# Attention with experts: softmax inverses and root guesses on ScalarE, root refinement on GpSimd, all q/k scaling on VectorE, input rows two batches ahead

## The chip, the cores and the metric

The kernel runs on one core of a Trainium2 chip. A core has five engines that run their own instruction queues side by side and meet through semaphores: TensorE (PE, matrix products), VectorE (DVE), ScalarE (ACT), GpSimd (POOL) and SyncE (SP, which here only issues DMAs). The metric is the time of one execution on the device, in microseconds (us); lower is better. Three runs of the kernel before took 1273.59, 1277.20 and 1277.99 us, median 1277.2 us.

## The reference, cut to what matters

16 batches of 256 tokens of width 256; 16 heads of 64 columns.

```
shift = silu(t) @ W_ada.T + b_ada
h = _ln(x, ln1_g, ln1_b) + shift
qkv = (h @ Wqkv.T).reshape(b, n, 3, H, HD)
q = _ln(qkv[:, :, 0].transpose(0, 2, 1, 3), qn_g, qn_b)      # mean and root over each head's 64 columns
k = _ln(qkv[:, :, 1].transpose(0, 2, 1, 3), kn_g, kn_b)
attn = softmax(einsum(q, k) / 8);  o = attn @ v
x = x + o @ Wout.T
gate = softmax(tok @ Wgate.T)                                # tok: all 4096 rows
vals, idx = top_k(gate.T, 512)                               # 512 rows for each of 8 experts
g = _ln(tok[idx], mlp_g, mlp_b)
y = gelu(g @ fc1 + b1s) @ fc2 + b2s
tok = tok.at[idx].add(y * vals)
```

`_ln` divides by sqrt(variance + 1e-5). The softmax divides by the sum of 256 exponentials.

## The kernel before, in words

The program has three parts. Attention runs to about 983 us of the span, the choice of rows for the experts to about 1072 us, and the eight experts to the end. The change touches the first part and one small piece of the second.

**Units.** `over_batches` walks over batches; each has eight units, `hp` 0 to 7, one for each pair of heads (`u` counts them all). Every engine has its own `batch` function with the same walk, and each queue's order is the order in which its function is written. Entries -1 and B (16) start and drain the pipeline; batches 2 to 14 are one loop body, the others are written out. In unit `hp`, TensorE transposes q and k of pair `hp+1` (L1272), forms a projection chunk of 512 columns in three passes (L452 to L454), multiplies the probabilities of pair `hp-1` by v (L1294) and sums them with a matrix of ones (L1298), forms the scores of pair `hp` (L1310, L1319), the rough scores of pair `hp+1` for their row maximum (L1330), and a second chunk. `CHUNKS` says which units have chunks: 0, 3, 4 and 7 a q and a k chunk each, 1 and 5 two v chunks, 2 and 6 none. Unit 0 has besides the output projection of the previous batch. Of the projected q and k, unit 7 of one batch and unit 0 of the next make one group (pairs 0 to 3), units 3 and 4 the other (pairs 4 to 7).

**Dividing by the softmax sum.** VectorE waits for the sum (`attended`), takes its reciprocal from PSUM into `rec` (L1147), multiplies (`oT`, L1149, which sets `divided`) and rounds a copy (`o_hi`, L1153); GpSimd forms the rest `o_lo` (L928). TensorE's next L1294 writes the same bank `av`, so it waits for `divided` of the unit before.

**Roots.** ScalarE copies each q or k chunk (`raw`, L966) and squares it (`sq`, L968); VectorE sums the squares by head (L1105). At the end of units 0 and 4, VectorE adds up `var` (L1189, L1191) and runs `rsqrt`: a guess from the bits and three Newton steps, eleven dependent instructions on 128x34 or 128x36 elements (L1023 to L1031). In units 1 and 5, after the maximum `m` (L1169), the four chunks of the group are scaled (`times_rstd`, L831): three on VectorE, one on GpSimd (`POOL_CHUNKS`). TensorE asks for them in units 3 and 7 (`qn_ready`, `qn_pool_ready` before L1272).

**Rows.** The same roots carry the variances of the batch's input rows (`xh`, L1139: x of the batch after, in unit 1) and of its result rows (`xh2`, L1089, unit 5, printed as xh in the profile). `sync_batch` loads `x_sb` one batch ahead. In the second part `last_rows` (L1093) does the same for the last batch, between the one-hot tables and the row lists.

Of the kernel before, what the change touches and what calls it, by code (L numbers as in the profile page):

```python
# [28 lines left out]
P = 128  # L29
# [20 lines left out]
NEWTON = 3  # L50
FIRST_LOOPED, LAST_LOOPED = 2, B - 2
# [26 lines left out]
def make_counts():  # L78
# [8 lines left out]
    for b in range(-1, B + 1):  # L87
# [53 lines left out]

class Need:
# [11 lines left out]
def over_batches(eng, batch):  # L154

    batch(-1, cur=False, nxt=True, prv=False)
    batch(0, cur=True, nxt=True, prv=False)
    batch(1, cur=True, nxt=True, prv=True)
    with eng.Fori(FIRST_LOOPED, LAST_LOOPED + 1) as b:
        batch(b, cur=True, nxt=True, prv=True)  # L160
    batch(B - 1, cur=True, nxt=False, prv=True)
    batch(B, cur=False, nxt=False, prv=True)


def build(nc, x, condT, w_adaT, vecs, w_qkvT, w_outT, w_gateT, experts, b2s, consts, out):
    ctx = ExitStack()
    with ctx:
# [38 lines left out]
        var_half = sb("var_half", [P, NH + 4], I32)  # L206
        ny = sb("ny", [P, NH + 4])
# [126 lines left out]
        tanh_done = sem("tanh_done")  # L334
# [27 lines left out]
        chunk_summed = sem("chunk_summed")  # L362
        rstd_ready = sem("rstd_ready")
        hT_split = sem("hT_split")
# [3 lines left out]
        dve_step = sem("dve_step")  # L368
        free_sem = {"act": act_read, "dve": dve_read}
# [150 lines left out]
        def phase23_pool(pool):  # L520
# [5 lines left out]
            nc.gpsimd.tensor_tensor(flat(w2_lo[0]), w2, flat(w2_hi[0]).bitcast(F32), ALU.subtract).then_inc(first_w2_lo_ready, 1)  # L526
            pool.wait_ge(index_ready, 1)
# [30 lines left out]
        def phase23_scalar(act):  # L558
# [22 lines left out]
            split_w2(0)  # L581
            act.wait_ge(first_transposed, 1)
# [243 lines left out]
        POOL_CHUNKS = 1  # L826

        def times_rstd(eng, par, c):

            r = rstd[par][:, c * 8:(c + 1) * 8].rearrange("p (h o) -> p h o", o=1).to_broadcast([P, 8, HD])  # L830
            return eng.tensor_tensor(qn[par][:, c, :].rearrange("p (h d) -> p h d", d=HD),  # L831
                                     raw[:, c, :].rearrange("p (h d) -> p h d", d=HD), r, ALU.mult)

        def sync_batch(sp):
            need = Need(sp)

            def batch(b, cur, nxt, prv):
                if nxt and not (isinstance(b, int) and b < 0):
                    need(xh_ready, b + 1)
                    sp.dma_start(x_sb[:, :, :], x[bass.ds(b + 1, 1)].rearrange("o (t p) d -> p (o t) d", p=P)  # L840
                                 if not isinstance(b, int) else x[b + 1].rearrange("(t p) d -> p t d", p=P)).then_inc(x_in, 16)
# [35 lines left out]
        def _(pool):  # L877
            need = Need(pool)
            nc.gpsimd.memset(ones[:, :], 1.0).then_inc(ones_ready, 1)
# [18 lines left out]
            def batch(b, cur, nxt, prv):  # L898
                def normalise(hp, c):

                    par = 1 if hp == 0 else 0
                    g = b * 2 + (1 if hp == 0 else 2)
                    if c == 0:
                        need(rstd_ready, through("newton", b, hp))
                        need(qk_transposed, (g - 1) * GU)
                    ins = times_rstd(nc.gpsimd, par, c)
                    if c == POOL_CHUNKS - 1:
                        ins.then_inc(qn_pool_ready, 1)

                for hp in range(UNITS):  # L910
# [13 lines left out]
                    if (cur and hp > 1) or (hp == 0 and prv):  # L924

                        for pair in ((hp - 2,) if hp else (UNITS - 2, UNITS - 1)):
                            need(normed, u - 1 if pair != UNITS - 1 else u)
                            nc.gpsimd.tensor_tensor(o_lo[:, pair, :], oT[pair % 2][:, :], o_hi[:, pair, :].bitcast(F32), ALU.subtract).then_inc(o_split, 1)  # L928
                    if hp == 1 and cur:
                        normalise(0, 0)  # L930
                    if hp == 5 and nxt:
                        normalise(4, 0)
# [4 lines left out]
            phase23_pool(pool)  # L937
# [3 lines left out]
        def _(act):  # L941
            need = Need(act)
            act.wait_ge(cond_in, 48)
# [462 lines left out]
```

## Time and profile before

| | value |
|---|---|
| median of three runs | 1277.2 us (1273.59 to 1277.99) |
| the profiled execution | 1278.72 us |
| its span in the trace | 1276.9 us |
| busy: TensorE, VectorE, ScalarE, GpSimd | 1102.1, 1050.9, 625.0, 565.7 us |
| share of the span | 86%, 82%, 49%, 44% |
| chain that ended last, by engine | TensorE 67%, VectorE 22%, issue 6% |
| granted TensorE clock, mean | 0.949 |

Busy time is the union of an engine's instructions; waiting is not in it. "Chain" is the path of work followed back from the last instruction: at each step to what released it. The duration of an instruction overlaps the next one's by about a tenth of a microsecond, so where instructions stand back to back, the distance of their starts is the better measure. A duration that is many times the shortest of its kind has a wait in it that the profiler does not show apart.

### The profile page before, as it was taken

The numbers are of one execution on the slowest core, as the hardware profiler recorded it, in microseconds if no ns is written. First come the engines' busy times: TensorE is split into PE (matmuls) and PEld (weight loads), VectorE is DVE, ScalarE is ACT, GpSimd is POOL, SyncE is SP. The second block draws the span as 40 slices with busy tenths as digits, with TensorE's granted clock in tenths as the row PEclk, the third lists the DMA queues.
The fourth block names the chain that finished last, engine by engine and source line by source line (L and its number), as shares of the span: only waits on it lengthen the run. The fifth ranks groups of instructions, "written<-read, shape, count | busy, mean of one in ns | idle before, by whom it ended". The sixth has DMA issues, their size and how long they took to land.

```text
span 1276.9 us, 24531 instructions
## 1 busy us (share of the span) xinstructions
PE 1102.1 (86%) x8291; PEld 849.3 (67%) x8291; DVE 1050.9 (82%) x1967; ACT 625.0 (49%) x1000; POOL 565.7 (44%) x507
## 2 busy tenths in 40 slices
PE   4689999999999999999999999999986015999996
PEld 3457676767767676767677676767664014898995
DVE  8688988888888989888888889898886884777773
ACT  4445655555464655555554646555541101544541
POOL 2465544454454545444444545444552203335423
PEclk9799999999999999999999999999998555999998
DMA  4000000000001000000000000000001403346412
GB/s 173 9 1 18 17 18 17 16 16 16 16 16 33 9 24 16 16 16 16 16 16 19 14 33 15 18 16 16 9 18 41 146 1 126 100 108 173 118 19 31
DMA packets 32277, 48.50 MB, mean 38 GB/s; under 512 B 7920, under 2 KB 28528, under 8 KB 30960
## 3 DMA queue, kind: packets, MB, share of 16 engines
q1 hardware_dynamic: 26096, 39.49, 9.5%
q0 software_dynamic: 6144, 8.52, 3.6%
q8 instruction: 23, 0.38, 0.1%
q14 instruction: 14, 0.11, 0.0%
HBM read 35.29 MB, written 12.71 MB: 38 GB/s over the span
## 4 chain that ended last, share of the span: by engine, by line
PE 67%; DVE 22%; issue 6%; ACT 1%; DMA 1%; POOL 0%; DVEq 0%; SPq 0%; ACTq 0%; POOLq 0%
PE ch L452 12%; PE ch L453 10%; PE ch L454 10%; PE av L1294 8%; PE sc L1319 7%; PE sc L1310 4%; DVE rec L1147 4%; PE av L1298 3%; PE pq L1272 3%; DVE qn L831 3%; PE mx L1330 2%; DVE var L1189 2%; DVE hit L706 1%; PE sc L452 1%; PE sc L453 1%
## 5 line engine op out<-in xcount | busy, mean ns | idle before, releaser
L923 POOL TENSOR_TENSOR qk_lo<-qkT,qk_hi 128x512 fp32r<-128x512 f32 x128 | 165.1, 1290 | 272.5 <-ACT qk_hi L989 272.5
L1147 DVE RECIPROCAL rec<-av 128x256 f32<-128x256 f32 x128 | 224.6, 1755 | 45.3 <-PE av L1298 44.8
L1001 ACT ACTIVATE prob<-sc 128x1024 f32<-128x1024 f32 x128 | 131.4, 1027 | 236.2 <-PE sc L1319 236.2
L918 POOL TENSOR_TENSOR prob_sum<-prob 128x512 f32<-128x512 f32 x128 | 165.0, 1289 | 140.5 <-ACT prob L1001 140.5
L452 PE MATMUL ch<-w_hi,hT_lo 128*128 128x512 f32 x384 | 173.8, 452 | 7.5 <-DVE w_lo L1069 7.2
L1294 PE MATMUL av<-prob,V 128*64 128x256 f32 x1024 | 141.0, 396 | 43.4 <-DVE oT L1149 41.0
L1169 DVE TENSOR_REDUCE m<-mx 128x4 bf16<-128x1024 f32 x128 | 155.5, 1214 | 0.0
L453 PE MATMUL ch<-w_lo,hT_hi 128*128 128x512 f32 x384 | 153.8, 401 | 0.0
L454 PE MATMUL ch<-w_hi,hT_hi 128*128 128x512 f32 x384 | 152.8, 398 | 0.0
L1294 PEld LDWEIGHTS av<-prob,V 128*64 128x64 f32 x1024 | 65.6, 137 | 101.2 <-issue 81.1
L1105 DVE TENSOR_REDUCE ssum<-sq 128x8 f32<-128x512 f32 x128 | 84.8, 680 | 54.8 <-ACT sq L968 53.0
L983 ACT ACTIVATE qkT<-pq,vec 128x256 f32<-128x256 f32 x128 | 72.2, 564 | 100.6 <-PE pq L1272 100.6
L928 POOL TENSOR_TENSOR o_lo<-oT,o_hi 128x256 fp32r<-128x256 f32 x128 | 94.6, 739 | 24.2 <-DVE o_hi L1153 24.2
L966 ACT ACTIVATE raw<-ch 128x512 f32<-128x512 f32 x128 | 75.4, 589 | 56.1 <-PE ch L454 55.9
L551 POOL DMA_INDIRECT out<-yout,index x32 | 52.3, 1634 | 106.3 <-DVE yout L822 99.9
L452 PEld LDWEIGHTS ch<-w_hi,hT_lo 128*128 128x128 f32 x384 | 73.2, 191 | 30.2 <-issue 8.3
L1272 PE MATMUL pq<-con,qn 128*128 128x128 f32 x512 | 79.3, 278 | 12.5 <-DVE qn L831 12.5
L1310 PE MATMUL sc<-neg_ident,m 128*128 128x256 bf16 x512 | 78.9, 277 | 12.1 <-issue 9.3
L454 PEld LDWEIGHTS ch<-w_hi,hT_hi 128*128 128x128 f32 x384 | 73.6, 192 | 19.6
L1319 PE MATMUL sc<-qk_hi,qk_lo 64*128 64x256 f32 x512 | 86.4, 334 | 0.0
L989 ACT ACTIVATE qk_hi<-qkT 128x512 fp32r<-128x512 f32 x128 | 80.7, 630 | 11.6
L595 ACT ACTIVATE yT<-ch,b_sb 128x512 f32<-128x512 f32 x64 | 44.1, 688 | 86.2 <-PE ch L454 86.1
(196 smaller groups left out, 2749.3 us busy)
## 6 DMA issues: line engine op xcount, KB each, us to landing
fcw<-experts SPq DMA_DIRECT2D x8, 2048.0 KB, 9.1
x_sb<-x SPq DMA_DIRECT2D x16, 256.0 KB, 2.8
xr_sb<-x SPq DMA_DIRECT2D x16, 256.0 KB, 2.7
out<-tok SPq DMA_DIRECT2D x16, 256.0 KB, 2.2
rows_dram<-xh SPq DMA_DIRECT2D x16, 256.0 KB, 2.2
prob<-w_qkvT SPq DMA_DIRECT2D x2, 512.0 KB, 8.2
qn<-w_qkvT SPq DMA_DIRECT2D x2, 512.0 KB, 9.0
V<-w_qkvT SPq DMA_DIRECT2D x2, 512.0 KB, 8.3
```

What stands on the lines that cost most here:

```text
L452: nc.tensor.matmul(psum, l_lo, r_hi, start=first, stop=False)
L453: nc.tensor.matmul(psum, l_hi, r_lo, start=False, stop=False)
L454: return nc.tensor.matmul(psum, l_hi, r_hi, start=False, stop=last)
L918: nc.gpsimd.tensor_tensor(prob_sum[(hp - 1) % 2][:, :, :], pr[:, :, 0, :], pr[:, :, 1, :], ALU.add).then_inc(prob_summed, 1)
L923: nc.gpsimd.tensor_tensor(qk_lo[par][:, :], qkT[par][:, :], qk_hi[par][:, :].bitcast(F32), ALU.subtract).then_inc(lo_ready, 1)
L1001: nc.scalar.activation(prob[hp % 2][:, :], sc[:, :], ACT.Exp, scale=HD ** -0.5).then_inc(prob_ready, 1)
L1147: chain(nc.vector.reciprocal(rec[:, :], av[:, N:2 * N]))
L1169: nc.vector.tensor_reduce(m[(hp + 1) % 2][:, :], mx[:, :].rearrange("p (a j) -> p a j", a=4), AX.X, ALU.max).then_inc(max_ready, 1)
L1272: ins = nc.tensor.transpose(pq[:, at * P:(at + 1) * P], qn[gpar][:, c, i * P:(i + 1) * P], ident)
L1294: nc.tensor.matmul(av[hh * HD:(hh + 1) * HD, 0:N], V[gpar][:, jt, i * P + hh * HD:i * P + (hh + 1) * HD], prob[(hp - 1) % 2][:, at:at + N] ...
L1310: nc.tensor.matmul(both[:, :, it, :], m[par][:, hh * TT + it:hh * TT + it + 1].to_broadcast([P, P]), neg_ident[:, :].rearrange("p (o n) -> ...
L1319: ins = nc.tensor.matmul(sc[:, at:at + N], k_part[par][rows, keys], q_part[par][rows, 0:N], start=False, stop=(k_part is qk_hi and q_part ...
```

## The change

- **Inverse of the softmax sum.** ScalarE waits for `attended`, takes the logarithm of the sum (`log_sum`) and then the exponential of its negative (`rec`). VectorE multiplies the sum by `rec` in place in PSUM (`error`), multiplies the product by `rec` (`o_raw`), and forms (error - 2) * o_raw: one Newton step, with the sign turned. The sign is taken back by a subtraction where `tok` is formed. The rounded copy `o_hi` is made by ScalarE, after `prob`.
- **Roots.** VectorE writes half the variance plus half of 1e-5, once, for all 36 columns; ScalarE guesses the inverse root by a logarithm and an exponential (`power_guess`); GpSimd makes one Newton step in four instructions (`refine`). All four chunks are scaled by VectorE (`normalise`), group (b,0) at the end of unit 0 instead of unit 1, group (b,4) still in unit 5.
- **Order.** On VectorE the maximum `m` stands between the two head sums of a unit instead of behind both. Result rows move from unit 5 to unit 6.
- **Rows ahead.** The statistics of x are taken in unit 3 for the batch after the next, and `xh` is written in unit 6; `x_sb` is loaded two batches ahead. The loop body covers batches 2 to 13.
- **Start and end.** silu of the condition uses an exponential and VectorE's reciprocal instead of a tanh; the last rows' root goes the same way through ScalarE and GpSimd.

```
-                        chain(nc.vector.reciprocal(rec[:, :], av[:, N:2 * N]))
+                        need(o_split, u - 2)
+                        need(inverse_ready, u)
                         o = oT[(hp - 1) % 2]
-                        nc.vector.tensor_tensor(o[:, :], av[:, 0:N], rec[:, :], ALU.mult).then_inc(divided, 1)
-                        nc.vector.tensor_copy(o_hi[:, (hp - 1) % UNITS, :], o[:, :]).then_inc(normed, 1)
+                        nc.vector.tensor_tensor(av[:, N:2 * N], av[:, N:2 * N], rec[:, :], ALU.mult).then_inc(error_done, 1)
+                        nc.vector.tensor_tensor(o_raw[:, :], av[:, 0:N], rec[:, :], ALU.mult).then_inc(rough_done, 1)
+                        need(error_done, u)
+                        need(rough_done, u)
+                        nc.vector.scalar_tensor_tensor(o[:, :], av[:, N:2 * N], 2.0, o_raw[:, :], ALU.subtract, ALU.mult).then_inc(divided, 1)
...
# ScalarE, in every unit, around prob
+                        need(attended, u)
+                        need(divided, u - 1)
+                        nc.scalar.activation(log_sum[:, :], av[:, N:2 * N], ACT.Ln).then_inc(log_done, 1)
+                        need(log_done, u)
+                        nc.scalar.activation(rec[:, :], log_sum[:, :], ACT.Exp, scale=-1.0).then_inc(inverse_ready, 1)
                     if cur:
                         nc.scalar.activation(prob[hp % 2][:, :], sc[:, :], ACT.Exp, scale=HD ** -0.5).then_inc(prob_ready, 1)
+                        need(divided, u)
+                        nc.scalar.activation(o_hi[:, (hp - 1) % UNITS, :], oT[(hp - 1) % 2][:, :], ACT.Copy).then_inc(o_hi_ready, 1)
...
+            def power_guess(b, hp, extra=0):
+                need(var_ready, count)
+                need(rstd_ready, count - 1)
+                nc.scalar.activation(log_var[:, 0:n], var[:, 0:n], ACT.Ln, scale=2.0).then_inc(log_var_done, 1)
+                need(log_var_done, count)
+                nc.scalar.activation(guess[:, 0:n], log_var[:, 0:n], ACT.Exp, scale=-0.5).then_inc(guess_ready, 1)
...
+            def refine(b, hp, extra=0):
+                need(guess_ready, count)
+                nc.gpsimd.tensor_tensor(a, y, y, ALU.mult).then_inc(pool_step, 1)
+                nc.gpsimd.tensor_tensor(a, a, v, ALU.mult).then_inc(pool_step, 1)
+                nc.gpsimd.tensor_tensor(a, three_halves[:, 0:n], a, ALU.subtract).then_inc(pool_step, 1)
+                need(qn_ready, b * 2 + (0 if hp == 0 else 1))
+                nc.gpsimd.tensor_tensor(dst, a, y, ALU.mult).then_inc(rstd_ready, 1)
...
+            def normalise(b, hp):
+                need(rstd_ready, through("newton", b, hp))
+                need(qk_transposed, (g - 1) * GU)
+                for c in range(4):
+                    ins = times_rstd(1 if hp == 0 else 0, c)
+                ins.then_inc(qn_ready, 1)
```

Three places of the queues are shown, all in batch 1, which is written out and has the loop's order. VectorE before, in unit 4, from the division to the start of the root:

```order
L1147 RECIPROCAL rec<-av 128x256
L1149 TENSOR_TENSOR oT<-av,rec 128x256
L1153 CAST o_hi<-oT 128x256
L1105 TENSOR_REDUCE ssum<-sq 128x8 x2
L1169 TENSOR_REDUCE m<-mx 128x4
L1189 TENSOR_SCALAR var<-ssum 128x32
L1191 TENSOR_SCALAR var<-mv 128x2
L1023 TENSOR_SCALAR var_half<-var 128x36
L1024 TENSOR_SCALAR ny<-var_half 128x36
```

The same stretch of VectorE's queue now, from the second instruction of the division on, with unit 5 behind it:

```order
L1217 TENSOR_TENSOR o_raw<-av,rec 128x256
L1220 SCALAR_TENSOR_TENSOR oT<-av,o_raw 128x256
L1178 TENSOR_REDUCE ssum<-sq 128x8
L1235 TENSOR_REDUCE m<-mx 128x4
L1178 TENSOR_REDUCE ssum<-sq 128x8
L1258 TENSOR_SCALAR var<-mv 128x4
L1261 TENSOR_SCALAR var<-ssum 128x32
L1216 TENSOR_TENSOR av<-av,rec 128x256
L1217 TENSOR_TENSOR o_raw<-av,rec 128x256
L1220 SCALAR_TENSOR_TENSOR oT<-av,o_raw 128x256
L1235 TENSOR_REDUCE m<-mx 128x4
L860 TENSOR_TENSOR qn<-raw,rstd 128x512 x4
```

The eleven instructions of the root and the rounded copy are gone from it, and the two multiplications and the subtraction of each unit stand in the place of the reciprocal.

ScalarE's queue before, in unit 4:

```order
L983 ACTIVATE qkT<-pq,vec 128x256
L985 ACTIVATE qkT<-pq,vec 128x256
L989 ACTIVATE qk_hi<-qkT 128x512
L966 ACTIVATE raw<-ch 128x512
L968 ACTIVATE sq<-ch 128x512
L1001 ACTIVATE prob<-sc 128x1024
L966 ACTIVATE raw<-ch 128x512
L968 ACTIVATE sq<-ch 128x512
```

And now:

```order
L1035 ACTIVATE qkT<-pq,vec 128x256
L1037 ACTIVATE qkT<-pq,vec 128x256
L1041 ACTIVATE qk_hi<-qkT 128x512
L1018 ACTIVATE raw<-ch 128x512
L1020 ACTIVATE sq<-ch 128x512
L1055 ACTIVATE log_sum<-av 128x256
L1057 ACTIVATE rec<-log_sum 128x256
L1061 ACTIVATE prob<-sc 128x1024
L1066 ACTIVATE o_hi<-oT 128x256
L1018 ACTIVATE raw<-ch 128x512
L1020 ACTIVATE sq<-ch 128x512
```

Three instructions are new in each unit: two before `prob`, one behind it that waits for VectorE, with the second chunk queued behind it.

GpSimd's queue now, in unit 5, where before one chunk was scaled behind `o_lo`:

```order
L957 TENSOR_TENSOR prob_sum<-prob 128x512
L962 TENSOR_TENSOR qk_lo<-qkT,qk_hi 128x512
L967 TENSOR_TENSOR o_lo<-oT,o_hi 128x256
L915 TENSOR_TENSOR na<-guess 128x36
L917 TENSOR_TENSOR na<-na,var 128x36
L919 TENSOR_TENSOR na<-three_halves,na 128x36
L924 TENSOR_TENSOR rstd<-na,guess 128x36
```

The four small instructions stand behind the two large ones of the unit.

## Rows read from the trace of the kernel before

**Rows 1.** Busy time by stretch: start:end us, length, each engine's busy time, clock.

```profile
60.00:117.00 57.00, 50.26 (x366) 36.65 (x367) 50.51 (x80) 28.55 (x48) 35.78 (x38) 0.94 0.02 6
117.00:931.00 814.00, 770.34 (x5924) 573.62 (x5923) 709.47 (x1249) 457.18 (x770) 391.94 (x364) 1.00 0.06 18
931.00:983.40 52.40, 41.96 (x346) 29.44 (x345) 39.70 (x63) 18.10 (x28) 23.10 (x22) 0.97 0.05 16
```

**Rows 2.** TensorE's waits, 39 to 985 us: total us, times, longest us.

```profile
PE av L1294 <- DVE oT L1149: 41.0, 26, 3.9
PE pq L1272 <- DVE qn L831: 12.5, 14, 9.3
PE sc L1310 <- issue: 9.3, 18, 0.7
```

**Rows 3.** Timeline of TensorE in one batch: start us, us, instruction, [idle before, releaser].

```profile
311.95 0.60 PE L1298 MATMUL av<-prob_sum,ones 128*64 128x256 f32 x4
...
325.55 1.08 PE L1294 MATMUL av<-prob,V 128*64 128x256 f32 x8 [2.23 <-DVE oT L1149]
...
329.99 0.66 PE L1272 MATMUL pq<-con,qn 128*128 128x128 f32 x4 [0.18 <-DVE qn L831]
```

**Rows 4.** Timeline of VectorE in the same batch, end of unit 4.

```profile
318.74 1.25 DVE L1189 TENSOR_SCALAR var<-ssum 128x32 f32<-128x32 f32 x1
320.02 0.65 DVE L1191 TENSOR_SCALAR var<-mv 128x2 f32<-128x2 f32 x1
...
323.07 0.20 DVE L1031 SCALAR_TENSOR_TENSOR rstd<-na,ny 128x36 f32<-128x36 f32 x1
```

**Rows 5.** Timeline of ScalarE, unit 4 and the start of unit 5.

```profile
310.25 0.57 ACT L983 ACTIVATE qkT<-pq,vec 128x256 f32<-128x256 f32 x1
...
311.90 0.58 ACT L966 ACTIVATE raw<-ch 128x512 f32<-128x512 f32 x1
...
314.06 1.03 ACT L1001 ACTIVATE prob<-sc 128x1024 f32<-128x1024 f32 x1 [1.08 <-PE sc L1319]
315.89 0.60 ACT L966 ACTIVATE raw<-ch 128x512 f32<-128x512 f32 x1 [0.81 <-PE ch L454]
...
316.86 0.57 ACT L983 ACTIVATE qkT<-pq,vec 128x256 f32<-128x256 f32 x1
```

**Rows 6.** Groups by line, whole span: busy us, mean ns, idle before.

```profile
L1147 DVE RECIPROCAL rec<-av 128x256 f32<-128x256 f32 x128 | 224.6, 1755 | 45.3 <-PE av L1298 44.8
L1169 DVE TENSOR_REDUCE m<-mx 128x4 bf16<-128x1024 f32 x128 | 155.5, 1214 | 0.0
L1105 DVE TENSOR_REDUCE ssum<-sq 128x8 f32<-128x512 f32 x128 | 84.8, 680 | 54.8 <-ACT sq L968 53.0
L923 POOL TENSOR_TENSOR qk_lo<-qkT,qk_hi 128x512 fp32r<-128x512 f32 x128 | 165.1, 1290 | 272.5 <-ACT qk_hi L989 272.5
L928 POOL TENSOR_TENSOR o_lo<-oT,o_hi 128x256 fp32r<-128x256 f32 x128 | 94.6, 739 | 24.2 <-DVE o_hi L1153 24.2
L1153 DVE CAST o_hi<-oT 128x256 fp32r<-128x256 f32 x128 | 64.0, 500 | 4.4
L1149 DVE TENSOR_TENSOR oT<-av,rec 128x256 f32<-128x256 f32 x128 | 54.3, 425 | 4.4
```

**Rows 7.** Timeline of VectorE: three scaled chunks in batch 0 and in a looped batch.

```profile
63.72 3.48 DVE L831 TENSOR_TENSOR qn<-raw,rstd 128x512 f32<-128x512 f32 x3
...
328.05 1.89 DVE L831 TENSOR_TENSOR qn<-raw,rstd 128x512 f32<-128x512 f32 x3
```

**Rows 8.** The chain that ended last, in the last batch.

```profile
967.27 1.03 ACT prob L1001
968.37 1.28 POOL prob_sum L918
969.70 0.65 PE av L1298 x4
```

**Rows 9.** Busy time of one looped batch at a lower clock.

```profile
524.10:582.30 58.20, 55.49 (x421) 41.17 (x420) 50.34 (x88) 32.67 (x55) 27.94 (x26) 0.97 0.06 18
```

More of the change, by code:

```diff
@@ L139, in slot_bank, with has_second, xh_before, rows_before @@
     return COUNTS["bank", b if isinstance(b, int) else FIRST_LOOPED, key]
+def has_second(b):
+    return not isinstance(b, int) or b + 2 < B
+def xh_before(b, hp):
+    if hp == 0:
+        return 0
+    return min(b + 2, B) if isinstance(b, int) else b + 2
+def rows_before(b, hp):
+    if hp == 0:
+        return 0
+    return b - 1
 class Need:
@@ L160, in over_batches @@
         batch(b, cur=True, nxt=True, prv=True)
+    batch(B - 2, cur=True, nxt=True, prv=True)
     batch(B - 1, cur=True, nxt=False, prv=True)
@@ L837, in batch @@
             def batch(b, cur, nxt, prv):
[L838 to L841, printed above, removed]
+                if has_second(b):
+                    need(xh_ready, b + 2)
+                    sp.dma_start(x_sb[:, :, :], x[bass.ds(b + 2, 1)].rearrange("o (t p) d -> p (o t) d", p=P)
+                                 if not isinstance(b, int) else x[b + 2].rearrange("(t p) d -> p t d", p=P)).then_inc(x_in, 16)
                 if prv:
@@ L926, in batch @@
                         for pair in ((hp - 2,) if hp else (UNITS - 2, UNITS - 1)):
-                            need(normed, u - 1 if pair != UNITS - 1 else u)
+                            need(o_hi_ready, u - 1 if pair != UNITS - 1 else u)
                             nc.gpsimd.tensor_tensor(o_lo[:, pair, :], oT[pair % 2][:, :], o_hi[:, pair, :].bitcast(F32), ALU.subtract).then_inc(o_split, 1)
[L929 to L932, printed above, removed]
+                    if hp == 0 and cur:
+                        refine(b, 0)
+                    if hp == 5 and (nxt or prv) and not (isinstance(b, int) and b == B):
+                        refine(b, 4)
                     if isinstance(b, int) and b == 0:
@@ L991, in batch @@
                         weights_high(0 if hp == 2 else 1)
+                    if hp == 5 and (nxt or prv) and not (isinstance(b, int) and b == B):
+                        power_guess(b, 4)
                     if live:
@@ L1170, in batch @@
                                                 AX.X, ALU.max).then_inc(max_ready, 1)
-                    if hp == 5 and prv and not last_entry:
-                        token_rows(b)
-                    if (hp == 1 and cur) or (hp == 5 and nxt):
-                        g = b * 2 + (1 if hp == 1 else 2)
-                        need(rstd_ready, through("newton", b, hp - 1))
-                        need(qk_transposed, (g - 1) * GU)
-                        for c in range(POOL_CHUNKS, 4):
-                            ins = times_rstd(nc.vector, 1 if hp == 1 else 0, c)
-                        ins.then_inc(qn_ready, 1)
+                    if hp in (0, 3, 4, 7) and (cur if hp < 2 else nxt):
+                        head_sums(b, hp, 1)
+                    if hp == 5 and nxt:
+                        normalise(b, 4)
+                    if hp == 6 and prv and not last_entry:
+                        token_rows(b)
+                    if hp == 6 and has_second(b):
+                        need(rstd_ready, through("newton", b, 4))
+                        if cur:
+                            need(slot_filled, through("slot", b, (1, 2)))
+                        else:
+                            need(slot_filled, through("slot", -1, (1, 2)))
+                        input_rows(rstd[0])
                     if hp == 2 and prv and not last_entry:
```

157 lines of the change are left out of this document (83 added, 74 removed).

## The prediction

> **What bounds the kernel now.** I read the busy time by stretch first. In the 14 batches between 117 and 931 us TensorE is busy 770.34 of 814.00 us and VectorE 709.47 [rows 1]: per batch 58.1 us, of which 55.0 and 50.7. ScalarE has 457.18 / 14 = 32.7 and GpSimd 28.0. (All by a 14th of these rows.) So TensorE stands still for 43.7 us in this stretch, 3.1 a batch, and every engine else has room. Then I read what ends TensorE's idle time. Between 39 and 985 us it waits 41.0 us for `oT`, 12.5 for the scaled q and k and 9.3 at the scores under "issue" [rows 2]; the reader is to see that the first two are VectorE by name. The third is VectorE too by my reading: the score product needs the maximum `m`, which is queued behind the division.
>
> The place is one per batch. TensorE stands 2.23 us before the value product at 325.55 and 0.18 before the transposes at 329.99 [rows 3]. VectorE's timeline beside it shows why: the two instructions for the variance take 1.25 and 0.65 us, the root follows and ends at 323.07 + 0.20 = 323.27 [rows 4], and only then come the reciprocal, 1.755, and the multiplication, 0.425 [rows 6], which end at 325.45; TensorE goes on at 325.55. So VectorE is late, not slow on average, and what the change takes off it in front of `divided` is worth up to 3.1 us a batch and no more, because 55.0 us of TensorE's work stay as they are.
>
> **What the parts cost, VectorE.** Removed per batch: 8 reciprocals at 1.755 = 14.0, 8 rounded copies at 0.500 = 4.0 [rows 6], two roots of eleven instructions, each from 320.67 (320.02 + 0.65) to 323.27, 2.6, together 5.2 [rows 4]. Added: the multiplication from PSUM is in the trace at 0.425 [rows 6]; three stand where one stood, 16 x 0.425 = 6.8. Two chunks more to scale: three take 1.89 in a looped batch [rows 7], 0.63 each, 1.3. Sum: 50.7 - 14.0 - 4.0 - 5.2 + 6.8 + 1.3 = 35.6 us of 55.
>
> **ScalarE.** A logarithm of 128x256 is not in the trace. Its nearest rows are the 0.57 for the same size with scale and bias from memory, as upper end, and the slope between 0.58 for 512 columns and 1.03 for 1024 [rows 5], which is 0.88 ns a column and gives 0.58 - 0.22 = 0.36 for 256, as lower end. I take 0.42 for the logarithm, the exponential and the copy alike, because like the lower pair they have no operands from memory but the tile. Per batch 24 x 0.42 = 10.1, and four small guesses of some 0.2: 32.7 + 10.1 + 0.8 = 43.6, at the upper end 47.2. Below 55, but this engine waits in the middle of its queue, so its unit must be walked through. From the transposed q and k to the next, its queue holds: three instructions, 310.25 to 311.90, 1.65; a chunk, 315.89 to 316.86, 0.97 [rows 5]; logarithm and exponential with a handoff each of 0.07 (968.37 against 967.27 + 1.03 [rows 8]), 0.98; VectorE's two multiplications and subtraction, 1.3 with its handoff 0.07, beside which `prob` runs (0.94 to the next start); the rounded copy 0.35; the second chunk 0.97. Sum 6.3 us. With 0.57 for each of the new three it is 6.75. TensorE's unit is 316.86 - 310.25 = 6.61. So at my value ScalarE keeps pace with 0.3 us to spare, and at the upper end it loses 0.15 a unit over the five long units 7, 0 and 3 to 5, and gets it back under the output projection of unit 0 and in units without chunks.
>
> The Trainium skill, ScalarE: Activation LUTs, "What ACT_TABLE_LOAD costs", gives 186 ns plus 0.833 ns a column without pointer operands: 0.40 us for 256 columns, and ScalarE's unit would be 6.2 us by it. The rows fit: 1024 columns give 1.04 by the rule, the trace has 1.03 [rows 5].
>
> **Is the lag harmless?** Put the end of the sums in unit 4 at 312.55 (311.95 + 0.60 [rows 3]). Before, ScalarE was ready for it at 312.9, since a chunk from 311.90 lasts 0.97. Logarithm and exponential end near 313.8, before the scores, whose `prob` started at 314.06 [rows 5]; so `prob`, which TensorE needs, moves by nothing. `divided` comes at 313.8 + 1.4 = 315.2, and TensorE wants it at the next value product, some 5.1 us after 312.55, at 317.7. Where units are short (2, without chunks) ScalarE falls behind by some 0.7 us; the value product of unit 3 then finds `divided` with some 0.4 us to spare. The rounded copy is hidden: only the output projection needs its rest. The maximum `m` is asked for 6.6 us after the sums, and comes at 2.7 + 0.7 + 1.2 = 4.6 [rows 6]; in unit 3 the row statistics stand in front (two passes of 256 columns and two small instructions, some 1.2 by the 0.425 for this size), and with the lag from unit 2 it is there at up to 6.5: the tightest place.
>
> **The roots.** The way is longer in engines, shorter in queues. In unit 4 the second square ends near 316.9 on ScalarE before, where the next instruction starts [rows 5], and some 0.5 later now; the head sum takes 0.7 [rows 6]; the two variance instructions 0.4 in the clear, 1.9 as in rows 4; the guess 0.6: at the latest 320.6. GpSimd has its two large instructions in front, 1.29 and 0.74 [rows 6], from about 316.86 + 1.65 + 0.1 = 318.6, and is free at 320.6 too. A small GpSimd instruction is not in the trace: 1.290 for 512 and 0.739 for 256 columns [rows 6] make 2.15 ns a column and 0.19 fixed, 0.27 for 36; the bounds are 0.19 and 0.739. Four with handoffs: 1.4 (1.0 to 3.2). So the root is ready near 322.0 and the four scales at 0.63 end at 324.5, with three at 3.48 as in batch 0 [rows 7] at 326.6. TensorE asks at 329.99 - 2.23 - 0.18 = 327.6 [rows 3]. They are in time by 1.0 to 3.1. Queued behind the scales is the division of unit 6, due 2 us later than they. In unit 0 the wait of VectorE for ScalarE and GpSimd stands in front of the scales with `tok` behind them, but TensorE is in the output projection there, 48 products of 256 columns. I cost the longer way at nothing; without that cover it is about 2 us a batch.
>
> At 63.72 three scales took 3.48 us beside GpSimd's work, against 1.89 at 328.05 [rows 7]. The Trainium skill, SBUF — State Buffer, "SBUF: two separate sides", has such a VectorE instruction and a GpSimd one excluding each other for a whole instruction; by it each of the four scales could stand behind a GpSimd instruction of 1.29 and the last end at 324.5 + 5.2 = 329.7, 2.1 too late, which is the second rival below. That the two slow each other the trace bears out; in the looped batch it is hardly there.
>
> **Rows two batches ahead.** It takes two instructions off unit 1 and puts them in unit 6, where VectorE has room; the load is earlier by a batch. I cost it at nothing, since TensorE's wait for input rows is not among the three large ones [rows 2].
>
> **The sum, against the profiled execution (1278.7 us, 1.5 above the median of the runs).** Between 117 and 931 us: 43.7 of idle time, of which I leave 0.3 us a batch for new small stalls (4.2): -39.5. Between 60 and 117 us TensorE is idle 57.0 - 50.3 = 6.7, and there are some waits ahead; three VectorE stalls go: -6. The last batch, without chunks, is idle 52.4 - 42.0 = 10.4 [rows 1]; its last units already go by the round scores, `prob`, `prob_sum`, sums, 969.70 + 0.65 - 967.27 = 3.1 plus the scores 1.5 (312.55 to 314.06 [rows 3, 5]), 4.6 a unit [rows 8], and ScalarE's queue without chunks is 6.3 - 1.9 = 4.4; the units ahead of them, now over 5 us, come down to that: -5. The start: one statistic more on VectorE, one exchange more for the root: +1. The last rows' root in the second part: 2.6 against some 2: -0.6. Total -50, so 1228.6 for such an execution and 1227 for the median.
>
> **Rivals.**
> - ScalarE sets the pace. For it: three added instructions and a wait in a queue of 6.3 to 6.75 us against 6.61. Price at 0.3 us in each of the six long units, 1.8 a batch, 14 batches: 25, 1252 us.
> - Late scales. For it: the doubled scales of batch 0 and GpSimd's unseen small instructions; with 0.739 each (+1.9) and the slow scales (+2.1) they end at 328.5, 0.9 too late, and the division behind them holds the next value product as much again: 2 us a batch, 28 in 14: 1255 us. Against it: both upper ends must hold.
> - The slower side: the exchange ScalarE, VectorE, ScalarE in every unit. ScalarE stands at the rounded copy until VectorE has divided, and the second chunk, the next q and k and the next logarithm stand behind it. It decides when ScalarE's unit passes (58.1 - 55.0) / 6 = 0.5 us above 6.61, that is 7.1. At 7.4, 0.8 us in six units is 4.8 a batch, 59.8 instead of 58.1: +24 in 14 batches, and the end gains nothing: 1300 us. Against it: it needs 1.1 us more than I sum up, for instance both new functions at 0.95.
> - TensorE gives some back by its clock: at 0.97 a batch's work is 55.49 [rows 9] instead of 55.0. Until now that was hidden in its idle time. In all batches that is 7 us: 1234 us. I count it inside the forecast's own range.
>
> **How the numbers follow.** Forecast 0.76, ScalarE's pace 0.10, late scales 0.08, slower 0.06. The forecast's own range is 1217 to 1242: 10 us below if no new stall remains and the first batches gain all, 15 above with the clock and 0.5 us more a batch. Toward the rivals I take 1254 as the upper end. The hard floor is TensorE's idle time gone altogether, about 1211. Faster by over 0.5% (below 1270.8, about what a measurement of this kernel can tell): the first three cases and a remainder, 0.92. Within 0.5%: 0.03. Slower: 0.05.
>
> **What would show it.** Right: a period of 55.0 to 55.5 us between two looped batches; TensorE's wait for `oT` near nothing; VectorE's busy time in a batch near 36, ScalarE's near 44; logarithm and exponential at 0.36 to 0.45; the scores' wait under "issue" gone. Wrong: TensorE's waits for `prob`, for `qk_hi` or for a chunk bank held by ScalarE (first rival); waits of the transposes in unit 7 for `qn` (second); ScalarE's copy `o_hi` with long idle time before it and a period above 58 (third).

## The result and the profile after

The changed kernel takes 1209.4 us (median of 4 runs, 1208.2 to 1210.5) against 1275.4 us for the kernel before (4 runs, 1272.6 to 1278.0): ratio 0.947, 95% interval 0.945 to 0.950. The forecast was 1227 us, with 1217 to 1242 as its own range and 1254 as the upper end toward the rivals: the sign and the place of the stall were right, the size was not. The time lies 7.6 us below 1217, and even below the "hard floor" of 1211. One execution of all, in experiment 2, took 5780 us with TensorE's products some four times as long, and it says nothing of its kernel.

I cut both profiled executions at the stores of the output rows. Up to the first store the time went from 117.7 to 112.9 us (-4.9), the 14 batches up to the fifteenth from 815.7 to 761.3 (-54.4), the last batch from 49.2 to 41.7 (-7.5), the rest from 294.3 to 291.4 (-2.9). The busy times of the stretches of after, to hold against [rows 1], and of one looped batch, against [rows 9]; columns as there:

```profile
112.86:874.18 761.32, 761.32 (x5939) 567.67 (x5937) 505.50 (x959) 585.73 (x1163) 402.58 (x449) 1.00 0.06 19
874.18:915.91 41.73, 36.15 (x314) 24.73 (x310) 19.56 (x41) 25.38 (x51) 22.88 (x25) 1.00 0.06 20
276.16:330.54 54.38, 54.38 (x427) 40.55 (x424) 36.30 (x69) 41.84 (x84) 28.80 (x33) 1.00 0.06 19
```

The first two numbers of a row are the point: in 14 batches TensorE, the first busy column, has no idle time at all, 54.38 us a batch. Before, between the same two stores, it was busy for 772.0 us, 55.14 a batch. So 43.7 us of idle time went, and 10.7 us of what the profile had as busy went with it. (Busy time counts an instruction to its end, and the ends of TensorE's products are modelled by the profiler.) VectorE is at 36.1 us a batch over the 14 (forecast 35.6), ScalarE at 41.8 (43.6).

What TensorE still waits for from 36 us to the end of the last batch, against [rows 2] (later waits belong to the second part):

```profile
PE pq L1336 <- DVE qn L860: 8.8, 2, 7.8
PE av L1362 <- POOL prob_sum L957: 7.9, 9, 4.3
...
PE av L1358 <- ACT prob L1061: 2.1, 4, 1.1
```

No `oT`, no "issue" at the scores. The waits that are left lie in batch 0 and in the last batch.

Instruction lengths, by line, against [rows 6] (busy us, mean ns | idle before), and ScalarE's timeline over one long unit, against [rows 5]:

```profile
L1216 DVE TENSOR_TENSOR av<-av,rec 128x256 f32<-128x256 f32 x128 | 55.2, 431 | 210.8 <-ACT rec L1057 210.8
L1235 DVE TENSOR_REDUCE m<-mx 128x4 bf16<-128x1024 f32 x128 | 155.4, 1214 | 0.8 <-PE mx L1394 0.8
L860 DVE TENSOR_TENSOR qn<-raw,rstd 128x512 f32<-128x512 f32 x128 | 121.8, 1009 | 36.1 <-POOL rstd L924 36.1
```

```profile
292.00 0.57 ACT L1035 ACTIVATE qkT<-pq,vec 128x256 f32<-128x256 f32 x1
...
294.60 0.39 ACT L1055 ACTIVATE log_sum<-av 128x256 f32<-128x256 f32 x1
295.02 0.42 ACT L1057 ACTIVATE rec<-log_sum 128x256 f32<-128x256 f32 x1
295.60 1.03 ACT L1061 ACTIVATE prob<-sc 128x1024 f32<-128x1024 f32 x1 [0.16 <-PE sc L1383]
296.86 0.42 ACT L1066 ACTIVATE o_hi<-oT 128x256 fp32r<-128x256 f32 x1 [0.23 <-DVE oT L1220]
...
298.40 0.57 ACT L1035 ACTIVATE qkT<-pq,vec 128x256 f32<-128x256 f32 x1
```

The logarithm takes 0.39 and the exponential 0.42 (taken: 0.42). From `qkT` to `qkT` it is 6.40 us, and in it ScalarE still waits 0.16 + 0.23 + 0.16 us by the brackets (the last is the chunk's, at 297.43). The 6.40 is TensorE's pace, since TensorE has no idle time; without the two waits for TensorE (0.16 each) ScalarE's own round is 6.1 us, where the prediction summed up 6.3.

One row above was not foreseen: a scale takes 1009 ns on average, not 0.63 us. The end of unit 4 and unit 5 on VectorE, with GpSimd beside it, against [rows 4, 7]:

```profile
299.15 0.16 DVE L1258 TENSOR_SCALAR var<-mv 128x4 f32<-128x4 f32 x1
299.27 0.18 DVE L1261 TENSOR_SCALAR var<-ssum 128x32 f32<-128x32 f32 x1
...
304.22 4.11 DVE L860 TENSOR_TENSOR qn<-raw,rstd 128x512 f32<-128x512 f32 x4
308.25 0.42 DVE L1216 TENSOR_TENSOR av<-av,rec 128x256 f32<-128x256 f32 x1
```

```profile
303.61 1.27 POOL L957 TENSOR_TENSOR prob_sum<-prob 128x512 f32<-128x512 f32 x1
306.30 1.48 POOL L962 TENSOR_TENSOR qk_lo<-qkT,qk_hi 128x512 fp32r<-128x512 f32 x1 [1.42 <-PE av L1362]
307.74 1.18 POOL L967 TENSOR_TENSOR o_lo<-oT,o_hi 128x256 fp32r<-128x256 f32 x1
```

Of the four scales the first takes 1.20 us and the fourth, put up at 306.55 behind `qk_lo`, 1.77:

```profile
306.55 1.77 DVE L860 TENSOR_TENSOR qn<-raw,rstd 128x512 f32<-128x512 f32 x1
```

It ends 0.5 us after `qk_lo` does; and `o_lo`, which takes 0.74 alone, starts at 307.74 and runs 1.18, 0.6 beyond the scale's end. The other two take 0.68 each, which is also the median. In these rows the two engines take turns by whole instructions. The Trainium skill has this rule (SBUF — State Buffer, "SBUF: two separate sides": "an exclusive lock, not a bandwidth split"), and the trace agrees. TensorE asks for these scales at 308.8, 0.5 us after they end: room, but less than the 1.0 to 3.1 us of the prediction.

The 1.25 and 0.65 us of the variance instructions in [rows 4] fit the same picture: here, with GpSimd idle beside them, they take 0.16 and 0.18, and in the kernel before they end at 319.99 and 320.67, each 0.02 to 0.04 us behind a large instruction of GpSimd:

```profile
318.68 1.27 POOL L923 TENSOR_TENSOR qk_lo<-qkT,qk_hi 128x512 fp32r<-128x512 f32 x1 [2.24 <-ACT qk_hi L989]
319.91 0.74 POOL L928 TENSOR_TENSOR o_lo<-oT,o_hi 128x256 fp32r<-128x256 f32 x1
```

So 1.6 us of what made VectorE late before was this.

### The profile page after: what moved, and what is told of

The parts are those of the page before. It is cut to its first block, busy times and chain, and to the rows that moved or that the text cites. A ratio compares the mean times of both kernels' runs of the same rounds, so it can differ in the third digit from the quotient of the medians.

```text
span 1207.3 us, 24525 instructions
## 1 busy us (share of the span) xinstructions
PE 1086.6 (90%) x8291; PEld 837.7 (69%) x8291; DVE 799.6 (66%) x1600; ACT 774.2 (64%) x1454; POOL 581.0 (48%) x616
## 4 chain that ended last, share of the span: by engine, by line
PE 84%; DVE 7%; POOL 3%; issue 2%; ACT 1%; DMA 1%; SPq 0%; DVEq 0%; POOLq 0%; ACTq 0%
PE ch L481 14%; PE ch L482 12%; PE ch L483 12%; PE av L1358 10%; PE sc L1383 9%; PE sc L1374 5%; PE pq L1336 5%; PE av L1362 5%; PE mx L1394 2%; DVE hit L737 2%; PE sc L481 1%; PE sc L483 1%; PE sc L482 1%; PE ch L1408 1%; PE ch L1321 1%
## 5 line engine op out<-in xcount | busy, mean ns | idle before, releaser
L962 POOL TENSOR_TENSOR qk_lo<-qkT,qk_hi 128x512 fp32r<-128x512 f32 x128 | 169.6, 1325 | 254.3 <-ACT qk_hi L1041 231.3
L1216 DVE TENSOR_TENSOR av<-av,rec 128x256 f32<-128x256 f32 x128 | 55.2, 431 | 210.8 <-ACT rec L1057 210.8
L1235 DVE TENSOR_REDUCE m<-mx 128x4 bf16<-128x1024 f32 x128 | 155.4, 1214 | 0.8 <-PE mx L1394 0.8
L860 DVE TENSOR_TENSOR qn<-raw,rstd 128x512 f32<-128x512 f32 x128 | 121.8, 1009 | 36.1 <-POOL rstd L924 36.1
L967 POOL TENSOR_TENSOR o_lo<-oT,o_hi 128x256 fp32r<-128x256 f32 x128 | 100.7, 786 | 26.2 <-ACT o_hi L1066 26.2
L1358 PEld LDWEIGHTS av<-prob,V 128*64 128x64 f32 x1024 | 62.1, 136 | 60.1 <-issue 38.5
```

Source lines behind the costliest of these rows:

```text
L860: return nc.vector.tensor_tensor(qn[par][:, c, :].rearrange("p (h d) -> p h d", d=HD), raw[:, c, :].rearrange("p (h d) -> p h d", d=HD), r ...
L962: nc.gpsimd.tensor_tensor(qk_lo[par][:, :], qkT[par][:, :], qk_hi[par][:, :].bitcast(F32), ALU.subtract).then_inc(lo_ready, 1)
L1235: nc.vector.tensor_reduce(m[(hp + 1) % 2][:, :], mx[:, :].rearrange("p (a j) -> p a j", a=4), AX.X, ALU.max).then_inc(max_ready, 1)
L1358: nc.tensor.matmul(av[hh * HD:(hh + 1) * HD, 0:N], V[gpar][:, jt, i * P + hh * HD:i * P + (hh + 1) * HD], prob[(hp - 1) % 2][:, at:at + N] ...
```

## The experiments

Twelve runs of eleven kernels, each the changed kernel with one edit; the edits are given in words, not as code. "Period" is the time from store to store in the loop; idle and busy are TensorE's a batch, over the 14 batches up to the fifteenth store.

**1. The inverse back on VectorE, nothing else.**

```
-  ScalarE: log_sum = Ln(av sums); rec = Exp(-log_sum); o_hi = copy(oT)
-  VectorE: av*rec, o_raw = av*rec, oT = (av*rec - 2) * o_raw
+  VectorE: rec = reciprocal(av sums); oT = av*rec; o_hi = copy(oT)
```

> Only the softmax inverse goes back to VectorE (reciprocal 1.755, multiplication 0.425, rounded copy 0.500, tok by addition); guessed and refined roots, four scales on VectorE and rows two batches ahead stay. Theory A (before, the root of 2.6 us in front of the division of unit 5 was the stall; TensorE's busy time holds a restart cost of each wait, so without waits it is 54.4 a batch): VectorE is at 36.3 - 24 x 0.43 + 8 x 2.68 = 47.4 us of a batch, has no root in front of the division, and the period comes out at 54.4 to 55.3, in all 1210 to 1225 us. Rival B (the reciprocals are what held TensorE): the 2.2 us wait for oT in unit 5 stays, period 56.5 or more, 1240 us or more.

Measured: 1208.8 us (ratio to before 0.947, 0.944 to 0.951), the time of the whole change. The stretch of 14 batches is the same to the hundredth, with VectorE at 47.2 us a batch:

```profile
114.56:875.88 761.32, 761.32 (x5939) 567.70 (x5937) 661.10 (x959) 468.86 (x827) 400.56 (x449) 1.00 0.06 19
```

So the half of the change that touches most instructions gives nothing once the roots are off VectorE. 128 reciprocals of 1.75 us stand in the kernel and the time is the same. Rival B falls.

**2 and 3. The roots back on VectorE (bit guess and three Newton steps), nothing else.** The profile below is of run 3, the same kernel once more.

```
-  ScalarE: log_var = Ln(var); guess = Exp(-log_var / 2)
-  GpSimd:  rstd = guess * (1.5 - guess*guess*var/2)
+  VectorE: shift, multiply-add, three rounds of three instructions
```

> Only the roots go back to VectorE (bit guess, three Newton steps, eleven instructions, 2.6 us); inverses by ScalarE, four scales on VectorE and rows two batches ahead stay. Theory A: the root stands in front of unit 5's division again, which is now 1.3 us instead of 2.2 and has ScalarE waiting behind it, so TensorE waits once a batch for oT, 2.2 - 0.9 = 1.3 us, plus up to 0.5 for the scales: period 55.5 to 56.2, in all 1226 to 1237 us, and TensorE's busy time is 0.1 to 0.4 us a batch above after's 54.38 for its restarts. Rival B: with the reciprocals gone there is room for the root, period within 0.3 of 54.4, 1209 to 1214 us.

> The kernel with the roots alone back on VectorE once more, for a profile (1241.95 us measured). Theory A: the 32.5 us over after are a wait for oT in unit 5 of each batch, 1.3 us or more, TensorE's busy time above 54.38 for the restart, and, since the division stands behind the root and ScalarE's rounded copy behind the division, one or two further waits: period about 56.5. Rival: the loss is spread over small waits in all units, as from ScalarE's pace.

Measured: 1241.95 us (ratio 0.974, 0.970 to 0.977) and 1242.9; period 56.4. Rival B falls here too. VectorE in unit 5, then the two TensorE rows of the batch that carry a wait:

```profile
307.10 0.18 DVE L1050 TENSOR_SCALAR var_half<-var 128x36 int32<-128x36 int32 x1 [0.28 <-DVE var L1238]
...
307.53 1.22 DVE L1053 SCALAR_TENSOR_TENSOR na<-ny 128x36 f32<-128x36 f32 x1
308.78 0.67 DVE L1054 TENSOR_TENSOR na<-na,var 128x36 f32<-128x36 f32 x1
309.48 0.20 DVE L1056 SCALAR_TENSOR_TENSOR ny<-na,ny 128x36 f32<-128x36 f32 x1
...
310.64 1.19 DVE L1054 TENSOR_TENSOR na<-na,var 128x36 f32<-128x36 f32 x1
311.87 0.20 DVE L1058 SCALAR_TENSOR_TENSOR rstd<-na,ny 128x36 f32<-128x36 f32 x1
...
312.83 0.42 DVE L1197 SCALAR_TENSOR_TENSOR oT<-av,o_raw 128x256 f32<-128x256 f32 x1
```

```profile
313.40 1.08 PE L1338 MATMUL av<-prob,V 128*64 128x256 f32 x8 [1.34 <-DVE oT L1197]
317.93 0.66 PE L1316 MATMUL pq<-con,qn 128*128 128x128 f32 x4 [0.33 <-DVE qn L857]
```

The wait for `oT` is 1.34 us, as theory A gave it. The root is not 2.6 us long but 5.0 from 307.10, since three of its small instructions, 1.22, 0.67 and 1.19 instead of 0.20, end with GpSimd's large ones, whose rows are

```profile
307.43 1.27 POOL L940 TENSOR_TENSOR qk_lo<-qkT,qk_hi 128x512 fp32r<-128x512 f32 x1 [2.23 <-ACT qk_hi L1005]
308.65 0.75 POOL L945 TENSOR_TENSOR o_lo<-oT,o_hi 128x256 fp32r<-128x256 f32 x1
310.50 1.28 POOL L935 TENSOR_TENSOR prob_sum<-prob 128x512 f32<-128x512 f32 x1 [1.10 <-ACT prob L1023]
```

The total is 5 us above theory A's range: of the 32.5 us over after, 25.8 lie in the 14 batches and 4.4 in the last one (46.2 us).

**4. Both back.**

> Both the inverse and the roots go back to VectorE; rows two batches ahead, the four scales on VectorE and the order stay. Theory A: both stalls of before are back and VectorE has one chunk a scaling more in front: period 58.0 to 59.5, in all 1270 to 1290 us, TensorE's busy time about 54.9 a batch again. Rival C (moving the rows out of unit 1 gave a good part): period below 57.5, under 1262 us.

Measured: 1267.0 us (ratio 0.993, 0.990 to 0.995). Neither expectation came as it stood. Theory A's total was 1270 or more; its period of 58.0 to 59.5 came in six of the 14 batches; they take 56.4 to 58.5, mean 57.7, where rival C wanted less than 57.5. The six are those at granted clock 0.97 (56.1 to 56.3 us busy); the others, at 1.00, take 56.4 to 57.4. The remaining parts (rows two batches ahead, four scales on VectorE, order) are worth some 0.6 us a batch, 8 to 10 us in all, where I had put nothing; between looped batches at clock 1.00 (57.4 and 58.2) it is 0.8. Which of the parts does it, no run separates. The four kernels make a square:

```
                      roots on VectorE     roots on ScalarE and GpSimd
inverse on VectorE          1267.0                 1208.8
inverse on ScalarE          1242.0                 1209.4
```

The roots bring 58 us by themselves, the inverse 25 by itself, and both together no more than the roots alone.

**5 and 6. One more copy on ScalarE in every unit, of 1024 and of 512 columns.**

```
   ScalarE: o_hi = copy(oT)
+  ScalarE: idle_out[:, 0:1024] = copy(w_hi)      (run 6: 512)
```

> The changed kernel with one more ScalarE copy of 1024 columns (about 1.03 us) behind the rounded copy of every unit; its result is used by nothing. ScalarE's unit goes from about 6.1 to 7.2 us, over TensorE's 6.57. Theory A: the period follows ScalarE only where units have two chunks, ScalarE's busy time is 41.8 + 8 x 1.03 = 50.1 of a batch: period 56.5 to 59, 1240 to 1275 us, TensorE waits at prob or chunk banks, and its busy time rises over 54.38 by 0.05 to 0.3 us for each wait. If the busy time is instead a property of the work (rival D: the shorter busy time of after comes from other contents, not from missing waits), it stays at 54.4 while the period rises.

> The changed kernel with one more ScalarE copy of 512 columns (about 0.6 us) behind the rounded copy of every unit. With 1024 columns (1.04 us) the period was 57.88 us, 7.24 a unit, with TensorE waiting. Theory A (ScalarE's queue, with its waits for VectorE, sets the pace from then on): 57.88 - 8 x 0.44 = 54.4, so the period stays between 54.4 and 55.0 and all takes 1209 to 1220 us. Rival (every ScalarE instruction in the exchange costs TensorE something at once): 54.4 + 3.5 x 0.6 / 1.04 = 56.4, 1237 us.

Measured: 1264.7 us, period 57.9 (ratio 0.991, 0.988 to 0.994), and 1226.2 us, period 55.3 (0.961, 0.958 to 0.963). The first, over 14 batches and in the four TensorE rows with a wait of one batch:

```profile
117.92:928.21 810.29, 779.61 (x5936) 568.18 (x5936) 506.39 (x960) 677.72 (x1275) 398.33 (x448) 1.00 0.06 18
```

```profile
291.49 0.50 PE L482 MATMUL ch<-w_hi,hT_lo 128*128 128x512 f32 x1 [0.50 <-DVE tok L1199]
297.19 0.50 PE L1397 MATMUL mx<-qk_hi 64*128 64x256 f32 x4 [0.27 <-ACT qk_hi L1042]
308.38 0.60 PE L1377 MATMUL sc<-neg_ident,m 128*128 128x256 bf16 x4 [0.66 <-issue]
321.27 0.65 PE L1365 MATMUL av<-prob_sum,ones 128*64 128x256 f32 x4 [0.53 <-POOL prob_sum L958]
```

This is the experiment on the floor. TensorE has the same instructions, at the same granted clock of 1.00, and is busy 779.61 / 14 = 55.69 us a batch instead of 54.38, with 2.19 idle. 1.3 us of busy time appears without any more work, and rival D falls. Besides the four waits the timeline has three stops of 0.04 to 0.15 us without a bracket, so it is some 0.2 us a stop. The rows show where most of it comes from: back to back, the durations overlap, and at a stop the overlap comes out. In after the value product of 1.08 us starts at 304.76 and the sums behind it at 305.68, 0.92 later; here it starts at 319.65, runs its whole 1.08 and is followed by the wait of 0.53. So the added busy time is partly how a stop is counted, but it was never work that keeps its length when the stop goes. For ScalarE, 8 x 1.04 us more a batch cost 3.5 and 8 x 0.6 us cost 0.9: its slack is 4 to 5 us a batch. Run 6 lies above theory A (period to 55.0, 1220 us) and far below its rival (56.4, 1237 us).

**7, 8 and 9. One, three and two more VectorE multiplications in front of the scales of unit 5.**

```
+  for extra in range(1):        (run 8: 3, run 9: 2)
+      VectorE: idle_out[extra] = w_hi[0] * w_hi[1]     (128x512)
   VectorE: four scales qn
```

> The changed kernel with one more VectorE multiplication of 128x512 (0.68 alone, up to 1.8 beside GpSimd) in front of the four scales of unit 5, in batches 0 and later. In after the scales end 0.7 us before TensorE wants them. Theory A (0.7 us is the whole slack there): the period rises by 0 to 0.9 us (up to 0.5 of a wait plus up to 0.3 of restart), in all 1209 to 1223 us. Rival (the scales had the 1.0 to 3.1 us of the prediction, or TensorE's order hides more): period 54.38, 1209 us, no wait for qn.

> The same with three such multiplications, 2.0 to 3.1 us. Theory A: TensorE waits once a batch for qn, 2.0 - 0.7 = 1.3 to 2.4 us, and its own busy time in a batch rises above 54.38 by 0.1 to 0.4 us, the restart of the one wait; period 55.8 to 57.2, in all 1229 to 1249 us. Rival D (busy time is a property of the work): busy time stays at 54.38 and the period rises by the wait alone.

> The changed kernel with two more multiplications in front of the four scales of unit 5. One gave a wait of 0.58 us a batch and a period of 55.12; three gave 2.8 us, and behind that wait TensorE ran 3 us at its lower clock, period 58.7 to 60.2. Theory E (the lower clock comes only behind a long wait): wait of 1.2 to 2.2 us, granted clock 1.00, busy time at most 0.3 over 54.38, period 55.8 to 56.9, 1228 to 1243 us. Rival (it grows evenly with the wait): busy time 1.0 or more over 54.38, period over 57.

Measured: 1221.1 us (ratio 0.957, 0.954 to 0.959), period 55.12; 1282.2 (1.005, 1.003 to 1.007), mean 59.2; 1263.4 (0.989, 0.986 to 0.992), mean 58.1. With one, theory A holds: a wait of 0.58 us, busy time up by 0.16 in such a batch. With two and three it does not. The waits, 2.2 and 2.8 us, are at or above the upper ends, and busy time rises by 1.5 and 2.0; for run 9 these are the numbers of its rival. TensorE in run 9, with two, and then in after, the same products:

```profile
324.42 1.06 PE L1413 MATMUL ch<-wg_sb,tokT 128*128 128x8 f32 x8
327.71 1.07 PE L1341 MATMUL pq<-con,qn 128*128 128x128 f32 x4 [2.23 <-DVE qn L861]
...
329.01 0.63 PE L483 MATMUL ch<-w_lo,hT_hi 128*128 128x512 f32 x1
329.43 0.63 PE L484 MATMUL ch<-w_hi,hT_hi 128*128 128x512 f32 x1
```

```profile
302.63 0.39 PE L482 MATMUL ch<-w_lo,hT_hi 128*128 128x512 f32 x1
302.87 0.39 PE L483 MATMUL ch<-w_hi,hT_hi 128*128 128x512 f32 x1
```

From the start of one product to the next it is 0.42 us behind the wait, and 0.24 in after: the lower level of 1.2 GHz, for some 3.5 us (granted clock 0.51 from 327.71 to 331.20), and 0.97 over the loop. Theory E, that only a longer wait does this, falls by this case's own rows: in [rows 3] a wait of the same 2.23 us, in front of the value product, has no slow products behind it. But in the same trace of before the same place, with a wait of 2.19 us, has them; the first of these rows is from the batch of [rows 3], the others from the one at 525 us:

```profile
327.08 0.60 PE L1310 MATMUL sc<-neg_ident,m 128*128 128x256 bf16 x4
...
558.21 1.08 PE L1294 MATMUL av<-prob,V 128*64 128x256 f32 x8 [2.19 <-DVE oT L1149]
...
559.75 1.02 PE L1310 MATMUL sc<-neg_ident,m 128*128 128x256 bf16 x4
```

The granted clock is 0.50 from 559.7 to 562.7 there. Of the batches with such a wait of 2.0 to 2.3 us the loop lost clock in 2 of 14 in before, in 6 of 12 in run 4 and in all 14 in run 9. Run 9 differs in that its wait follows the eight gating products of 8 columns (1.06 us), where in the other two the wait comes ahead of them. That this raises the odds is a guess from these counts; it cannot be all, since in before and in run 4 the same order gives both outcomes. What decides stays open.

**10 and 11. Another order in the last batch.**

```
   only where b == B - 1:
-  TensorE: value product, scores, maximum products
+  TensorE: scores, (run 11: maximum products,) value product
-  ScalarE: logarithm, exponential of it, prob
+  ScalarE: prob, logarithm, exponential of it
   run 11 also, VectorE: m ahead of the division
```

> The changed kernel with another order in the last batch alone: TensorE computes a unit's scores ahead of the value product of the unit before, and ScalarE its exponential of the scores ahead of the logarithm. In after the last batch takes 41.7 us of which TensorE works 36.2; its units of 4.57 us go by the round scores, prob, prob_sum, sums. Theory (that round is what bounds the last batch): with prob_sum beside the next scores the round falls away, the last batch comes to 37 to 39 us, in all 3 to 5 us faster than after, 1204.5 to 1206.5. Rival (prob alone, or VectorE's maximum, is next in line): under 1.5 us gained.

> The last batch alone in another order, again from the changed kernel: scores and maximum products ahead of the value product on TensorE, the exponential ahead of the logarithm on ScalarE, and now the maximum m ahead of the division on VectorE (in the run before, m stood behind the division, the round went sums, logarithm, division, m, scores, 8.0 us a unit, and the batch took 59.8 us). Theory: TensorE's own work, some 4.2 us a unit, sets the last batch: 37 to 39.5 us instead of 41.7, in all 2 to 4.5 us faster than after. Rival (ScalarE's queue with the wait for the division in front of q and k is next): 41.5 us or more, nothing gained.

Measured: 1226.5 and 1220.4 us, 17 and 11 us slower than after; the last batch takes 59.8 and 54.1 us. The rivals hold, with more than they said. The rows of after from which I had argued:

```profile
890.79 1.02 ACT L1061 ACTIVATE prob<-sc 128x1024 f32<-128x1024 f32 x1 [0.62 <-PE sc L1383]
891.89 1.27 POOL L957 TENSOR_TENSOR prob_sum<-prob 128x512 f32<-128x512 f32 x1 [0.67 <-ACT prob L1061]
```

and run 11, ScalarE and TensorE:

```profile
900.81 0.42 ACT L1076 ACTIVATE o_hi<-oT 128x256 fp32r<-128x256 f32 x1 [1.42 <-DVE oT L1239]
...
902.91 0.80 PE L1415 MATMUL mx<-qk_hi 64*128 64x256 f32 x4 [2.19 <-ACT qk_hi L1041]
```

ScalarE stands for the division, and the next q and k stand behind it. This is the slower side's rival of the prediction, the exchange ScalarE, VectorE, ScalarE; with the order of after it costs nothing in the loop. TensorE's granted clock over this batch is 0.84, and its busy time 42.0 us, for 36.2 in after. In run 10 the waits are at the scores (12.4 us in six), where `m` stands behind the division.

**12. The same order with the inverse on VectorE, where ScalarE has no such wait.**

> The softmax inverse on VectorE as in the first experiment (1208.8 us, last batch 41.3), and in the last batch alone TensorE's scores and maximum products ahead of the value product and VectorE's m ahead of the division. ScalarE's queue there is q, k and prob, 2.8 us a unit, with no wait for a division in it, which is what took 54.1 us in the run with the inverse on ScalarE. Theory: TensorE's own work of some 4.2 us a unit sets the last batch: 37 to 39.5 us, in all 1204.5 to 1207, 2 to 4 us below the changed kernel. Rival (VectorE with 3.9 us a unit in one queue, or its m, is late now): 41 us or more, nothing gained.

Measured: 1211.9 us (ratio 0.950, 0.948 to 0.952), last batch 43.1 us: nothing gained, the rival holds. VectorE and GpSimd:

```profile
890.51 0.42 DVE L1217 TENSOR_TENSOR oT<-av,rec 128x256 f32<-128x256 f32 x1
890.83 1.28 POOL L962 TENSOR_TENSOR qk_lo<-qkT,qk_hi 128x512 fp32r<-128x512 f32 x1 [1.18 <-ACT qk_hi L1041]
890.97 1.29 DVE L1221 CAST o_hi<-oT 128x256 fp32r<-128x256 f32 x1
```

The rounded copy takes 0.29 us alone and 1.29 behind `qk_lo`. From one reciprocal to the next VectorE takes 4.6 us (888.73 to 893.31), longer than the 4.2 of TensorE's own work. That is the length of a unit in after too. Besides, TensorE waits 3.16 us for `oT` at 909.45, and the batch has a granted clock of 0.96. No kernel here beats 1208.8 us.

## Why the prediction was wrong, step by step

**The bound and its place: right.** One stall a batch, where the root stands in front of the division on VectorE. Experiments 1 to 4 show it: with the roots away the reciprocals do no harm, and with the roots back the wait for `oT` is back.

**"55.0 us of TensorE's work stay as they are": this step failed.** It took TensorE's busy time for its work. The work is 54.38 us. Before, 55.14 were busy between the stores, 0.76 a batch more, 10.7 us in all; some 2.4 of it is clock, for two of the 14 batches ran at 0.97, 56.1 and 56.2 us busy against 54.9 in the others; [rows 9] lies across the first of them. The rest stands beside waits, and experiments 5 and 7 show that this is what waits do, at granted clock 1.00: busy time goes up with them, by 0.16 us for one, by 1.3 for four and three small stops; before had four, and 0.6 more than after in a batch at clock 1.00. The "hard floor" of 1211 us hung on the same step, and the lower end of the range on that.

**"0.3 us a batch for new small stalls", 4.2 us: did not come.** With the 10.7 above, 14.9 us: the loop gave 54.4, forecast 39.5, of 69.6 in all against 50 by the profiled executions.

**The last batch: 7.5, not 5.** Not the units of 4.6 us, which came as said (4.57 at 888.64 and 893.22), but what went with them: a wait of 3.9 us for `oT` at 962.95 with the value product behind it at 1.97 us instead of 1.08, in a stretch at granted clock 0.97. I had counted that short.

**The second part: 2.9, not 0.6.** The root chain of the last rows is 0.17 us shorter, not 0.6. The row statistics there take 3.3 us instead of 6.8, but that need not be the change: with the same two instructions there they take 2.9 us in run 12 and 8.8 in run 6, and the stretch behind the last store takes 290.0 to 294.4 us over the profiles of the experiments. The 2.9 lie inside this scatter, and its cause stays open.

**The start: 4.9 against 6 less 1.** Right, by the total; no run separates its parts.

**ScalarE, by the sum of its queue: right within 0.2 us.** The sum was 6.3 (its terms as printed add up to 6.2), the round without the waits for TensorE is 6.1, and experiments 5 and 6 put its slack at 0.5 to 0.6 us a unit, where the prediction had 0.3.

**The scales: in time, by another sum, and so in part by luck.** GpSimd's small instructions take 0.26 us (taken: 0.27), the root was ready early, and the scales took 4.1 us for 2.5. "In the looped batch it is hardly there" read three scales at a moment when GpSimd was nearly idle. The second rival had 2.1 us for this and wanted 1.9 more; the first came to 1.6, the second not at all. Experiment 7 spent the slack with one instruction.

**The inverse: not priced by itself, and worth nothing once the roots are moved.** The prediction never summed the change without it. The root's 2.6 us taken away, against waits of 2.23 and 0.18 [rows 3], would have pointed to it.

**The rows two batches ahead: "I cost it at nothing".** Beside the old stalls some 8 us, together with the scales and the order (experiment 4).

## What to carry to other kernels

TensorE's busy time beside waits is not its floor: take the floor from a stretch without waits. For a change in several parts, ask of each whether the stall goes without it; here a root of eleven tiny instructions held what 128 large ones were blamed for. Small elementwise VectorE instructions on SBUF operands, next to large GpSimd ones, should be priced at up to the length of the latter.

## What was not expected of the hardware

- A 36-column instruction on VectorE took 0.20 us or 1.2, a rounded copy of 256 columns 0.29 or 1.29, a scale of 512 columns 0.68 or 1.77, by whether GpSimd was in a large instruction. Reductions (`m`, 1214 ns, and `ssum`, 681) and the multiplication with a PSUM operand (431) kept their means.
- A wait of 2.2 us was followed by some 3 us at TensorE's lower level in one batch and by none in the next, at the same place with the same work around it (experiment 9). The length of a wait does not tell its whole price.
- Two row statistics of 256 columns took 2.9 to 8.8 us in the second part, by kernel, with the same instructions.
